# Attention on one core: the causal mask as part of VectorE's row maximum, head by head, instead of as matrix products, and the negation as a 3-operand instruction

## What is computed

```python
B, T, C = x.shape            # 8, 512, 256; H = 16 heads, latent width L = 32
q_for_k = q_lat @ wqk_w.T + wqk_b
att = jnp.einsum('bhql,bhkl->bhqk', q_for_k, k_lat) * L ** (-0.5)
causal = jnp.tril(jnp.ones((T, T), dtype=bool))
att = jnp.where(causal[None, None], att, -jnp.inf)
att = jax.nn.softmax(att, axis=-1)
y_lat = jnp.einsum('bhqk,bhkl->bhql', att, v_lat)
```

## Time and profile before

| | |
|---|---|
| median of the runs | 1364.07 us (1362.13 to 1367.33) |
| profiled execution | 1364.51 us, of which the span of the core is 1362.4 us |
| PE busy | 1224.1 us (90%), 7222 matmuls |
| PEld busy | 948.7 us (70%) |
| DVE busy | 821.0 us (60%), 1331 instructions |
| ACT busy | 673.8 us (49%) |
| POOL busy | 449.3 us (33%) |
| `tensor_reduce`, line 948 | 197.8 us in 192 instructions, mean 1040 ns |
| mask products, line 1223 | 90.9 us in 352 matmuls, mean 258 ns |

### The profile page before, as it was taken

The page is one execution under the profiler, slowest core; times in us unless marked ns, Lnnn a source line. Parts: engine busy times, 40 slices in busy tenths (PEclk is TensorE's granted clock), DMA queues, the critical chain, the costliest instruction groups (busy, mean ns, idle before and its releaser), DMA issues.

```text
span 1362.4 us, 19910 instructions
## 1 busy us (share of the span) xinstructions
PE 1224.1 (90%) x7222; PEld 948.7 (70%) x7222; DVE 821.0 (60%) x1331; ACT 673.8 (49%) x1028; POOL 449.3 (33%) x335
## 2 busy tenths in 40 slices
PE   3479999999999999986489999996799999998996
PEld 3355666666666666653378888885588888887885
DVE  2567787878787878751277777774444444442343
ACT  0125556565656565652467777772555555540111
POOL 3254555555555555421000000000344444431000
PEclk9889999999999999995699999998799999999998
DMA  3064445454545454611203333333654555553671
GB/s 119 1 140 110 110 110 140 110 141 110 141 110 141 110 141 94 155 35 46 77 32 111 115 114 119 119 103 120 246 163 162 162 162 162 165 196 101 210 251 48
DMA packets 121774, 170.31 MB, mean 125 GB/s; under 512 B 47009, under 2 KB 76130, under 8 KB 121698
## 3 DMA queue, kind: packets, MB, share of 16 engines
q1 hardware_dynamic: 121378, 168.78, 42.7%
q10 hardware_dynamic: 320, 0.52, 0.1%
HBM read 72.26 MB, written 37.75 MB: 81 GB/s over the span
## 4 chain that ended last, share of the span: by engine, by line
PE 50%; DVE 4%; ACT 2%; DMA 1%; POOL 1%; issue 1%; SPq 0%; ACTq 0%; POOLq 0%; DVEq 0%
PE ring L357 7%; PE ring L358 7%; PE ring L359 7%; PE ring L1398 6%; PE tail L357 3%; PE tail L359 3%; PE tail L358 3%; PE tail L1398 2%; PE ring L1325 2%; PE ring L1308 1%; PE ring L1315 1%; PE tail L1249 1%; PE ring L1269 1%; PE ring L1238 1%; ACT x L720 1%
## 5 line engine op out<-in xcount | busy, mean ns | idle before, releaser
L948 DVE TENSOR_REDUCE mx<-ring 128x4 f32<-128x512 f32 (+2 forms) x192 | 197.8, 1040 | 80.6 <-PE ring L1223 79.8
L701 ACT ACTIVATE pt<-ring 128x1024 f32<-128x1024 f32 (+1 forms) x192 | 169.2, 882 | 143.7 <-PE ring L1238 130.9
L618 POOL TENSOR_SCALAR_AFFINE_SELECT pt<-pt 128x512 f32<-128x512 f32 x128 | 81.3, 635 | 240.1 <-ACT pt L701 240.1
L1221 PE MATMUL ring<-qks 96*128 96x384 f32 (+3 forms) x512 | 138.2, 359 | 5.1 <-DMA qks<-stg 4.3
L1238 PE MATMUL ring<-qks 98*128 98x256 f32 (+3 forms) x512 | 130.6, 358 | 7.3 <-DVE mx L948 3.0
L1238 PEld LDWEIGHTS ring<-qks 98*128 98x128 f32 x512 | 77.1, 194 | 65.2 <-DVE mx L948 27.6
L641 POOL TENSOR_TENSOR hl<-hid,hh 128x512 fp32r<-128x512 f32 x64 | 82.6, 1302 | 78.4 <-ACT hh L787 78.4
L1249 PE MATMUL tail<-pt,va 128*32 128x512 f32 (+3 forms) x1024 | 98.7, 458 | 6.7 <-POOL pt L618 6.6
L1221 PEld LDWEIGHTS ring<-qks 96*128 96x128 f32 x512 | 91.0, 197 | 14.9 <-ACT pt L701 5.9
L627 POOL TENSOR_TENSOR zl<-z,zh 128x1024 fp32r<-128x1024 f32 x8 | 19.3, 2411 | 245.2 <-ACT zh L740 245.2
L1062 DVE SCALAR_TENSOR_TENSOR hid<-ring,bias_e,gate 128x512 f32<-128x512 f32 x64 | 47.9, 748 | 83.4 <-ACT gate L781 47.2
(11 more groups left out here) (215 smaller groups left out, 3068.5 us busy)
## 6 DMA issues: line engine op xcount, KB each, us to landing
qks<-stg SPq DMA_DIRECT2D x384, 128.0 KB, 2.4
c_dram<-c2s SPq DMA_DIRECT2D x32, 512.0 KB, 5.2
c<-c_dram SPq DMA_DIRECT2D x32, 512.0 KB, 6.2
sl_dram<-sls SPq DMA_DIRECT2D x32, 256.0 KB, 3.4
sl<-sl_dram SPq DMA_DIRECT2D x16, 512.0 KB, 4.7
wg<-in_wg SPq DMA_DIRECT2D x16, 512.0 KB, 5.5
wu<-in_wu SPq DMA_DIRECT2D x16, 512.0 KB, 6.3
wd<-in_wd SPq DMA_DIRECT2D x16, 512.0 KB, 7.0
```

The costliest lines, as they stand in the source:

```text
L618: nc.gpsimd.affine_select(out=m, in_=m, compare_op=ALU.is_ge, fill=0.0, base=0, pattern=[[0, GH], [1, P]], channel_multiplier=-1).then_inc ...
L701: nc.scalar.activation(pt[j % 2][:, h:h + heads, 0:n], heads_of(tile, heads, n), ACT.Exp, scale=SCALE).then_inc(empty, 1)
L948: nc.vector.tensor_reduce(out=mx[:, g, i, h:h + heads], in_=heads_of(tile, heads, (i + 1) * P), axis=AX.X, op=ALU.max).then_inc(empty, 1)
L1221: nc.tensor.matmul(scores[:, h, :], qks[0:KS_ROWS, g, h0 + h, 0, i * P:(i + 1) * P], qks[0:KS_ROWS, g, h0 + h, 1, 0:n], start=(h == k), st ...
```

## The change

The product with `maskb` goes. A table `cmask` (128 x 512, f32) holds 384 columns of zeros and then the triangle of -1e30, so that its last n columns are the mask of a head with n keys. DVE now works head by head: one `tensor_tensor_reduce` adds the mask, writes the masked scores back to PSUM and keeps the running maximum. The negation gets a third operand, a table of zeros.

```diff
-    maskb = place("maskb", [P, GH, P], bf16)
+    cmask = place("cmask", [P, T], f32)
...
+    zeros = place("zeros", [P, NT, GH], f32)
...
-            nc.gpsimd.affine_select(out=maskb[:, :, :], in_=maskb[:, :, :], compare_op=ALU.is_ge, fill=MASKED, base=0,
-                                    pattern=[[0, GH], [-1, P]], channel_multiplier=1).then_inc(pool_ready, 1)
+            nc.gpsimd.affine_select(out=cmask[:, T - P:T], in_=cmask[:, T - P:T], compare_op=ALU.is_ge, fill=MASKED, base=0,
+                                    pattern=[[-1, P]], channel_multiplier=1).then_inc(pool_ready, 1)
...
-                    nc.vector.tensor_reduce(out=mx[:, g, i, h:h + heads], in_=heads_of(tile, heads, (i + 1) * P), axis=AX.X,
-                                            op=ALU.max).then_inc(empty, 1)
+                    n = (i + 1) * P
+                    scores = heads_of(tile, heads, n)
+                    for k in range(heads):
+                        last = nc.vector.tensor_tensor_reduce(out=scores[:, k, :], in0=scores[:, k, :], in1=cmask[:, T - n:T], scale=1.0, scalar=MASKED,
+                                                              op0=ALU.add, op1=ALU.max, accum_out=mx[:, g, i, h + k:h + k + 1])
+                    last.then_inc(empty, 1)
...
-                    blink(nc.vector.tensor_scalar(out=negmax[:, g, :, 0, :].bitcast(f32r), in0=mx[:, g, :, :], scalar1=-1.0,
-                                                  scalar2=None, op0=ALU.mult))
+                    blink(nc.vector.scalar_tensor_tensor(out=negmax[:, g, :, 0, :].bitcast(f32r), in0=mx[:, g, :, :], scalar=-1.0,
+                                                         in1=zeros[:, :, :], op0=ALU.mult, op1=ALU.add))
...
-                    bank = max(T // n, 1)
-                    for k in range(0, heads, bank):
-                        some = min(bank, heads)
-                        for h in range(k, k + some):
-                            nc.tensor.matmul(scores[:, h, :], qks[0:KS_ROWS, g, h0 + h, 0, i * P:(i + 1) * P],
-                                             qks[0:KS_ROWS, g, h0 + h, 1, 0:n], start=(h == k), stop=False)
-                        last = nc.tensor.matmul(scores[:, k:k + some, i * P:n], identb[:, :], maskb[:, 0:some, :], start=False, stop=True)
+                    for h in range(heads):
+                        last = nc.tensor.matmul(scores[:, h, :], qks[0:KS_ROWS, g, h0 + h, 0, i * P:(i + 1) * P],
+                                                qks[0:KS_ROWS, g, h0 + h, 1, 0:n], start=True, stop=True)
```

More of the change, by code:

```diff
@@ L335, in block_kernel @@
     SETUP_ACT, SETUP_PE = NC, 7
-    POOL_SETUP = 9
+    POOL_SETUP = 10
     LOADS = 21
@@ L571, in _ @@
             nc.gpsimd.memset(identb[:, :], 0.0).then_inc(pool_ready, 1)
-            nc.gpsimd.memset(maskb[:, :, :], 0.0).then_inc(pool_ready, 1)
+            nc.gpsimd.memset(cmask[:, :], 0.0).then_inc(pool_ready, 1)
             nc.gpsimd.memset(ones[:, :], 1.0).then_inc(pool_ready, 1)
-            pool.wait_ge(pool_ready, 4)
+            nc.gpsimd.memset(zeros[:, :, :], 0.0).then_inc(pool_ready, 1)
+            pool.wait_ge(pool_ready, 5)
             for m in (ident, identb):
@@ L585, in _ @@
                                     pattern=[[-HD, P // HD], [0, HD]], channel_multiplier=1).then_inc(pool_ready, 1)
-            pool.wait_ge(pool_ready, 8)
+            pool.wait_ge(pool_ready, 9)
             nc.gpsimd.affine_select(out=g3, in_=g3, compare_op=ALU.is_ge, fill=0.0, base=HD - 1,
@@ L589, in _ @@
             nc.gpsimd.memset(va[:, :, :, HD:L], 1.0).then_inc(pool_ready, 1)
-            pool.wait_ge(pool_ready, 10)
+            pool.wait_ge(pool_ready, 11)
             nc.gpsimd.memset(fp(qks[KS_ROWS:KS_ROWS + 2, :, :, 1, :]), 1.0).then_inc(pool_ready, 1)
```

## The result

The changed kernel takes 1388.5 us in the median (1386.5 to 1393.4), the kernel before 1365.7 in the same series: a ratio of 1.0176, 95% interval 1.0140 to 1.0211. It is 22.8 us slower, where 9 us less was forecast. The profiled execution has a span of 1384.8 us (before 1362.4) and a mean granted clock of 0.945 (before 0.958).

What follows compares the result with a forecast made beforehand. PE was taken as the bound, DVE close behind. Middle batches -0.8 us each (-5 over six), first -3, last -1.5: sum -9 from the profiled 1364.5, median forecast 1355 us, range 1332 to 1402.

Steps and rivals of the forecast that it cites:

- light stretch: Rest of a middle batch, 38.3 us: DVE's added 4.2 us fits its spare time, PE gains 2.7 us.
- the negation: Line 956 on DVE: still waits for POOL's line 599, edit costs nothing; starting later covers 0.46 us per group.
- heads: Mask and maximum head by head on DVE: 0.15 us fixed cost each, 2.0 us more per group.
- PE's saving: Dropped mask products on PE: 1.25 us per group, 5.0 per batch, where PE is the bound.
- dense stretch: 388.31 to 417.85 in a middle batch, both engines full: grows 1.9 us, PE's gain lost as DVE is the bound.
- rivals 1 and 2: DVE's price per head is 0.21 us (1366 to 1385) or 0.33 (1385 to 1410); chance 0.17 each.
- half rate: Writing scores back into the PSUM bank being read: +5.4 us per group more, 1470 and above; chance 0.05.
- rival 2: DVE's accumulator read does not overlap, 0.33 us per head: +6 us per batch, 1385 to 1410; chance 0.17.
- rival 3's first half: 3-operand negation does not wait for POOL, DVE wins 1.7 us per group: 1324; whole rival's chance 0.14.
- First and last batch: PE's gain counts for about 3 us in the first; longer DVE units leave 1.5 in the last.

Runs made afterwards that it cites:

- bias_moved: The changed kernel with POOL's bias sum moved later, behind the subtraction of line 610: 1370.1 us, ratio to before 1.0034.
- flip: The kernel before plus a useless 320-column DVE reduction ahead of the first group's cosine product, from batch 2 on: 1385.9 us, ratio 1.0143.
- after_rot: The changed kernel with POOL's sine product placed earlier and the bias sum left in place: 1366.6 us, ratio 1.0008.
- unmasked: The kernel before without PE's mask products and nothing in their place, row maximum over all keys: 1351.8 us, ratio 0.9889.
- dve_moved: The changed kernel with POOL's bias sum moved later and PE's mask products put back: 1379.4 us, ratio 1.0089.
- neg_only: The kernel before with only the new 3-operand negation: 1366.0 us, ratio 0.9994.
- flip_control: The kernel before with the same useless DVE reductions, but ahead of the second group's cosine product: 1365.7 us, ratio 1.0003.
- before_bias: The kernel before with only POOL's bias sum placed later: 1365.4 us, ratio 0.9994.

## Why the prediction was wrong

**The failed step is that of the light stretch**: "PE gains what its 13 units saved, 2.7 us", because DVE has "more than 10 us of spare time" there. Two things were wrong in it.

First, I counted spare time and did not ask what each moment of delay meets. I did ask it of the negation (its four heads make it start 0.46 us later under line 599: 0.41 measured, 1838 to 1428 ns). Of the cosine product I did not, though it has two SBUF inputs too, and I had used its row to say what such a product does under one of POOL's. The unit of 4 x 128 ahead of it grew from 0.60 to 0.99 us; its lead was 0.27. In place of -2.7 us the light stretch of batch 4 gave +4.3 (0.5 and 3.8), and +2.9 in the mean of the six middle batches. `bias_moved` and `flip` show that the race is 18 to 21 us of the result, and `after_rot` agrees. The Trainium skill, page SBUF — State Buffer, section Who interferes with whom, has the rule: a DVE instruction with two SBUF inputs shares a read port with GpSimd, and the order of issue decides which of the two blocks. The trace agrees at both ends (3.23 us for DVE, or 3.36 for POOL). Nothing in my rivals covers it.

Second, the value of time saved on PE and added on DVE was wrong even without the race. PE's saving is worth little even with no race and no new work on DVE: 13.9 us instead of 40 (`unmasked`), and about 9.3 beside the heads, where the sum had counted 20.7 (6 x 2.7, 3 and 1.5). The windows of the six middle batches in `unmasked`, `bias_moved` and `dve_moved`:

```profile
153.50:551.70 398.20, 376.00 (x2356) 249.60 (x2352) 324.19 (x485) 236.09 (x348) 223.65 (x175) 0.99 0.51 127
155.90:566.10 410.20, 379.45 (x2360) 248.46 (x2352) 346.72 (x1109) 236.93 (x347) 217.03 (x175) 0.99 0.50 123
158.10:578.30 420.20, 401.06 (x2596) 262.59 (x2616) 348.23 (x1109) 238.29 (x347) 216.99 (x175) 1.00 0.49 121
```

In `unmasked` PE's busy time falls by 24.7 us (from 400.73), not far from the 30 that 1.25 us in 24 groups make, so the products were priced about right. But the stretch shrinks by only 9.3, because PE's idle time grows from 6.8 to 22.2 us: the saving comes back as waits. A PE that is busy 98% of a batch is not one whose every saved 0.1 us counts. And the heads are not free where DVE has time. Group by group, means over the six middle batches in us per batch, from the starts of the negations:

| | light (groups 1 and 2) | forecast | dense (groups 3 and 4) | forecast |
|---|---|---|---|---|
| heads (before to `dve_moved`) | +1.3 | 0 | +0.8 | +1.9 |
| PE's saving (`dve_moved` to `bias_moved`) | -0.9 | -2.7 | -0.7 | 0 |
| the race (`bias_moved` to the changed kernel) | +2.5 | 0 | +0.4 | 0 |

The forecast's light and dense stretches are not cut quite at the groups, but the picture does not hang on that. Which loop of steps sets the group's length, I did not settle; that it is not the negation alone is shown.

**The heads.** Forecast 0.15 us each, measured about 0.12, within the ends given; per group about +1.4 instead of +2.0 (DVE's busy time in group 1 of batch 4 goes from 13.02 to 14.54 us, of which 0.2 is a longer wait of the negation). So rivals 1 and 2, with 0.21 and 0.33 and half rate, were wrong in mechanism although 1388 lies where rival 2 had put it. The Trainium skill's fixed latency per instruction (VectorE: DVE Perf Modes, TRN2 errata), an estimate of 0.125 us per head, comes close to what main instruction and read cost together.

**The dense stretch** was to grow by 1.9 us; groups 3 and 4 of batch 4 lost 0.5 instead, and in the mean of the six middle batches they grew by 0.5. The heads cost less there than forecast, and PE's gain, which I had called lost since DVE is the bound, paid most of it back.

**The negation** costs nothing and gives nothing: right, with `neg_only` at 0.9994 and rival 3's first half refuted.

**First and last batch.** Forecast -3 and -1.5. The first gives +5.1, in `bias_moved` +5.0 and in `unmasked` +3.3, each with a granted clock of 0.88 to 0.90 where it was 1.00. The clock was no part of my sum at all. But only a part of this belongs to the change. In `flip_control`, which issues the same instructions there as the kernel before, this batch takes 64.2 us at 0.95, and in `before_bias` 65.8 at 0.92, so the 60.7 us at 1.00 of the earlier trace rows was at the short end. What does go with the missing mask products is group 1: 15.1 to 15.2 us, with a stretch at half clock, in `unmasked`, `bias_moved` and the changed kernel, 13.2 before. The last batch gives -0.8. Attention starts 1.7 us sooner, but that is no proof of a lighter setup: in `neg_only`, whose setup is not lighter, the first negation comes at 88.9 us, 3.2 sooner than before. The first batch of `bias_moved`, of `unmasked`, and then of `flip_control` and `before_bias`:

```profile
90.10:155.90 65.80, 59.39 (x322) 38.62 (x322) 51.32 (x161) 32.14 (x45) 30.65 (x25) 0.88 0.48 114
```

```profile
89.50:153.50 64.00, 57.03 (x318) 37.49 (x322) 46.20 (x55) 31.99 (x45) 31.25 (x25) 0.90 0.50 117
```

```profile
92.30:156.50 64.20, 58.38 (x356) 37.68 (x364) 46.42 (x56) 32.08 (x45) 29.97 (x25) 0.95 0.49 117
90.40:156.20 65.80, 59.98 (x356) 38.70 (x364) 46.28 (x56) 32.15 (x45) 30.12 (x25) 0.92 0.49 114
```

The sum as it should have been: the heads +14.1, PE's saving -9.3, together +4.8 (1365.4 to 1370.1, before rounding) with the lost clock inside, and the race +18.3. The forecast had +11.4 (6 x 1.9) for the heads, -20.7 for PE and nothing for the race. Even without the race the change would not have paid. (The kernel before took 1365.7 and 1364.7 us in the series compared, so a sum across series is good to about 1 us.)

## What to carry to other kernels

When an edit makes one engine later by some tenths of a microsecond, look through the trace for every two-input DVE product that now starts near a POOL product, and compare the lead it had with the delay: a lead of 0.27 us was worth 18 to 21 us here. An engine's busy share of 98% does not price its saved time, and another's idle time does not make its new work free; leave its work out in one run, and the run says what the rest can be worth. A step that is put earlier can free one wait and lengthen the next (6.3 us for the negation became 14 more for `pt`), so read the engine's whole list of waits, not the one that was meant.

## What the runs showed of the hardware

- The main instruction of a head reads and writes the same PSUM bank at about one element per 1.0 ns (0.25 us from start to start for 128 elements, 0.62 to 0.64 for 512). Fixed are some 0.12 us per head, the accumulator's read (0.14 us in its row) included.
- Two products of 128x1024 with both inputs in SBUF, one on DVE and one on POOL: DVE's takes 3.23 us when it starts 0.2 us behind POOL's, and 1.22 where POOL's is out of the way; POOL's takes 3.36 when it starts 0.27 us behind DVE's, and 2.37 when it is first.
- The granted clock is not told by PE's idle time in a group alone. In `flip` a group in which PE was idle 2.5 us (17.33 busy of 19.80) stood at 0.91, and the sixth, idle 0.3 us, at 1.00. But in the changed kernel a group in which it was idle 3.3 us (14.74 busy of 18.00) stood at 1.00. No run changed PE's idle time by itself.
- A third operand in SBUF neither helps nor hurts the negation; freed of POOL it takes 175 ns in the old form and 176 in the new one, in the median.
